# Graph network kernel: tile-end comparisons as ScalarE signs, and GpSimd arithmetic moved

## What is computed

```
h = relu(layernorm(x));  x = x + SAGE(h, src, dst)            # three rounds of mean over neighbours
h = relu(layernorm(x));  x = x + MLP(h, mean attr by src, mean attr by dst)
h = relu(layernorm(x));  x = x + GATv2(h, src, dst)           # attention over incoming edges
h = relu(layernorm(x));  x = x + TP(h, attr, src, dst, type)  # messages of scalars and vectors
```

## Time and profile before

| | us |
|---|---|
| median of 3 runs | 2131.21 (2128.32 to 2134.73) |
| the profiled execution, its own time | 2126.57 |
| its span, first to last instruction | 2124.8 |
| VectorE (DVE) busy in it | 1753.1, 83% |
| TensorE (PE) busy | 1610.9, 76% |
| ScalarE (ACT) busy | 1103.9, 52% |
| GpSimd (POOL) busy | 977.8, 46% |

### The profile page before, as it was taken

One profiled execution on the slowest core, in us unless ns is written; L12 is line 12 of the kernel. 1 busy time (PEld: TensorE's weight loads), 2 busy tenths in 40 slices (PEclk: granted clock), 3 DMA queues, 4 the chain that ended last, 5 costly groups with the idle time before them and its releaser, 6 DMA issues.

```text
span 2124.8 us, 36111 instructions
## 1 busy us (share of the span) xinstructions
PE 1610.9 (76%) x8603; PEld 1273.5 (60%) x8603; DVE 1753.1 (83%) x5207; ACT 1103.9 (52%) x2865; POOL 977.8 (46%) x969
## 2 busy tenths in 40 slices
PE   4656668999998987455777777778377888788786
PEld 3222248888888974344776676677355555555555
DVE  8999988998998977787687787886767778778776
ACT  2787767888997963011423424245434444444443
POOL 4200001111221200577777777760057777777772
PEclk9887779999999998675978869789668787887878
DMA  5665668868886870343222222220021111111111
GB/s 181 197 192 162 181 196 326 308 225 292 323 305 246 327 261 29 110 109 82 71 76 70 79 73 73 75 64 1 32 70 56 54 56 55 55 55 55 55 55 48
DMA packets 168625, 280.38 MB, mean 132 GB/s; under 512 B 23985, under 2 KB 137272, under 8 KB 158578
## 3 DMA queue, kind: packets, MB, share of 16 engines
q1 hardware_dynamic: 132816, 191.61, 27.1%
q0 software_dynamic: 34368, 85.62, 13.4%
q10 hardware_dynamic: 1250, 0.86, 0.2%
HBM read 224.22 MB, written 53.79 MB: 131 GB/s over the span
## 4 chain that ended last, share of the span: by engine, by line
POOL 32%; DVE 13%; issue 12%; PE 11%; ACT 1%; DMA 1%; DVEq 0%; POOLq 0%; ACTq 0%
POOL G L750 19%; POOL AT L738 6%; POOL SCR L738 4%; PE PS L1995 2%; POOL EI L738 2%; PE PS L1996 2%; PE PS L1971 1%; DVE HOT_R L1252 1%; POOL G L738 1%; PE PS L1886 1%; DVE GROUPED_R L1267 1%; DVE GROUPED_R L1261 1%; DVE SCR L1426 1%; PE PS L1770 1%; PE PS L1947 0%
## 5 line engine op out<-in xcount | busy, mean ns | idle before, releaser
L750 POOL DMA_INDIRECT G<-table,src_idx x415 | 406.0, 978 | 167.3 <-issue 125.9
L2102 PE MATMUL PS<-SCR,OH 128*128 128x256 f32 x830 | 281.9, 504 | 107.8 <-DVE SCR L1723 104.7
L2102 PEld LDWEIGHTS PS<-SCR,OH 128*128 128x128 f32 x830 | 201.4, 252 | 160.3 <-DVE SCR L1723 120.7
L1886 PE MATMUL PS<-ALL_R 128*128 128x256 f32 (+3 forms) x2025 | 265.6, 288 | 22.8 <-DVE ALL_R L1314 8.1
L727 POOL DMA_INDIRECT HOT_R<-group_table,EI x56 | 63.3, 1130 | 467.0 <-PE PS L1850 252.3
L1971 PE MATMUL PS<-RX,OH 128*128 x830 | 178.4, 372 | 130.4 <-DVE SCR L1426 80.2
L1886 PEld LDWEIGHTS PS<-ALL_R 128*128 128x128 f32 (+1 forms) x2025 | 250.5, 189 | 25.6 <-issue 9.6
L1971 PEld LDWEIGHTS PS<-RX,OH 128*128 128x128 f32 x830 | 149.3, 248 | 160.2 <-issue 155.4
L738 POOL DMA_INDIRECT AT<-table,src_idx x208 | 213.8, 1028 | 63.4 <-issue 62.2
L957 ACT COPY SCR<-PS 128x640 f32<-128x640 f32 x83 | 57.5, 692 | 287.7 <-PE PS L2077 287.7
L1846 PE MATMUL PS<-HOT_R,GROUPED_R 128*119 128x448 f32 x776 | 181.9, 374 | 9.3 <-DVE G L1272 8.7
(11 more groups left out here) (430 smaller groups left out, 3883.2 us busy)
## 6 DMA issues: line engine op xcount, KB each, us to landing
ALL_R<-adjacency SPq DMA_DIRECT2D x72, 1600.0 KB, 7.5
adjacency<-ALL_R SPq DMA_DIRECT2D x26, 1600.0 KB, 7.6
AT<-dst_in_block SPq DMA_DIRECT2D x103, 128.0 KB
G<-table,src_idx POOLq DMA_INDIRECT x463, 2.5
AT<-table,src_idx POOLq DMA_INDIRECT x208, 2.9
table<-RX SPq DMA_DIRECT2D x10, 320.0 KB, 2.7
radial_rows<-SCR POOLq DMA_DIRECT2D x4, 512.0 KB, 5.7
SCR<-table,src_idx POOLq DMA_INDIRECT x111, 2.8
```

What stands on the lines that cost most here:

```text
L750: pool.indirect_dma_start(G[:, p, q, :], None, tables[i], bass.IndirectOffsetOnAxis(ap=src_idx[:, VB * k + q:VB * k + q + 1], axis=0)).the ...
L1886: ins = pe.matmul(PS[0:m, n % 2, 0:2 * w], (adj(slot) if slot is not None else first_adj(b))(c, m), both(i % 2, c, w), start=j == 0, stop= ...
L2102: ins = pe.matmul(PS[:, q, 0:MSG], OH[:, p, q, :], view(SCR, M_AT + (p * VB + q) * MSG, [[1, MSG]]), start=True, stop=True)
```

## The change

It has four parts.

- The counts: ScalarE writes, for each group, the sign of (visit - 0.5 - end) over 391 ends, five operations for the built visits and four for the others. VectorE sums the signs and makes the count with one affine operation (0.5 x sum + NT/2). The comparisons L1083 and L1114 and the four separate reductions L1115 go; L1097 reads the signs; one reduction over all four groups takes the place of L1115.
- The group table (L710, L712): ScalarE makes it as relu(1 - |row - index|), right behind the signs, and stores it from its own queue. The table's memory overlaps the ring of attributes, so GpSimd waits for that store before its second attribute gather.
- The integer source indices (L706, L707): ScalarE makes them inside its pair loop.
- The marks (L702, L703): GpSimd waits for `kinds_ready` instead of `valid_made`. The kind fills are ordered so that the marks' fills come last, and TensorE waits for the marks only there.

```diff
@@ fills
-        FILLS = attr_fills(range(2)) + [(g, j) for g in range(VG) for j in range(2)] + attr_fills(range(2, VG))
+        FILLS = attr_fills(range(2)) + [(g, j) for j in range(2) for g in range(VG)] + attr_fills(range(2, VG))
@@ gpsimd
             for g in range(VG):
                 at = bass.IndirectOffsetOnAxis(ap=tvi[:, g:g + 1], axis=0)
+                if g == 1:
+                    pool.wait_ge(s("groups_stored"), 16)
                 if g == ATTR_RING:
                     pack_block_words()
                     pool.wait_ge(s("fill_turned"), 5)
...
-            pool.wait_ge(s("valid_made"), 1)
+            pool.wait_ge(s("kinds_ready"), 1)
...
             pool.wait_ge(s("fill_copied_act"), N_FILL)
-            pool.tensor_copy(view(EI, 2 * VW + 3, [[VB, NB]]).bitcast(I32), view(EI, 2 * VW + 3, [[VB, NB]])).then_inc(s("idx_made"), 1)
-            pool.tensor_copy(src_idx[:], EI[:, 0, 0:NV + 1]).then_inc(s("idx_made"), 1)
-            pool.wait_ge(s("idx_made"), 2)
-            for c in range(4):
-                pool.tensor_scalar(view(SCR, HIGH0_AT + c * NSRC, [[1, NSRC]]), iota_h[:, 0:NSRC], bv[:, c:c + 1], None, ALU.is_equal).then_inc(s("groups_made"), 1)
-            pool.wait_ge(s("groups_made"), 4)
-            pool.dma_start(group_table.rearrange("(c p) n -> p c n", p=P), view(SCR, HIGH0_AT, [[NSRC, 4], [1, NSRC]])).then_inc(s("groups_stored"), 16)
...
             pool.wait_ge(s("block_summed"), FIRST)
+            pool.wait_ge(s("idx_made"), 2)
@@ scalar
             act.wait_ge(s("constants_made"), 11)
+            def rank(to, at, n, source):
+
+                for g in range(n):
+                    ins = act.activation(to[:, g], source, ACT.Sign, bias=half_below[:, at + g:at + g + 1], scale=-1.0)
+                ins.then_inc(s("ranked"), 1)
+
+            act.wait_ge(s("scalars_made"), 3)
+            act.wait_ge(s("merge_spread"), 1)
+            rank(built_ranks, VG, GA, PS[:, 2, 0:NT])
+            act.wait_ge(s("ends_spread"), 1)
+            rank(ranks, 0, VG, PS[:, 0, 0:NT])
+            for c in range(4):
+                ins = act.activation(view(SCR, HIGH0_AT + c * NSRC, [[1, NSRC]]), iota_h[:, 0:NSRC], ACT.Abs, bias=bv[:, c:c + 1], scale=-1.0)
+            ins.then_inc(s("groups_made"), 1)
+            act.wait_ge(s("groups_made"), 1)
+            act.activation(view(SCR, HIGH0_AT, [[1, 4 * NSRC]]), view(SCR, HIGH0_AT, [[1, 4 * NSRC]]), ACT.Relu, bias=1.0, scale=-1.0).then_inc(s("groups_made"), 1)
+            act.wait_ge(s("groups_made"), 2)
+            act.dma_start(group_table.rearrange("(c p) n -> p c n", p=P), view(SCR, HIGH0_AT, [[NSRC, 4], [1, NSRC]])).then_inc(s("groups_stored"), 16)
             copy_fills(0, KINDS_AT)
...
+                if j == NORM_FROM + NBLK:
+                    act.copy(view(EI, 2 * VW + 3, [[VB, NB]]).bitcast(I32), view(EI, 2 * VW + 3, [[VB, NB]])).then_inc(s("idx_made"), 1)
+                    act.copy(src_idx[:], EI[:, 0, 0:NV + 1]).then_inc(s("idx_made"), 1)
@@ vector
-            dve.tensor_copy(bv[:], stvi[:])
+            dve.tensor_copy(bv[:], stvi[:]).then_inc(s("scalars_made"), 1)
+            dve.wait_ge(s("scalars_made"), 1)
+            dve.tensor_scalar(half_below[:, 0:VG], tv[:, 0, :], 0.5, None, ALU.subtract).then_inc(s("scalars_made"), 1)
+            dve.tensor_scalar(half_below[:, VG:VG + GA], bv[:], 0.5, None, ALU.subtract).then_inc(s("scalars_made"), 1)
...
-            dve.tensor_tensor(cmp[:, 0:GA], view(PS, 2 * 512, [[0, GA], [1, NT]]), view(bv, 0, [[1, GA], [0, NT]]), ALU.is_lt)
...
-            dve.tensor_reduce(view(stv, 0, [[1, GA]]), cmp[:, 0:GA], AX, ALU.add)
+            dve.wait_ge(s("ranked"), 1)
+            dve.tensor_reduce(stv[:, 0, :], built_ranks, AX, ALU.add)
...
+            done(dve.tensor_scalar(stv[:, 0, :], stv[:, 0, :], 0.5, NT / 2, ALU.mult, ALU.add))
...
-            dve.wait_ge(s("ends_spread"), 1)
-            for g in range(VG):
-                done(dve.tensor_scalar(H[:, g * 4:g * 4 + 4, :].rearrange("p a b -> p (a b)")[:, 0:NT], PS[:, 0, 0:NT], tv[:, 0, g:g + 1], None, ALU.is_lt))
-                done(dve.tensor_reduce(tv[:, 1, g:g + 1], H[:, g * 4:g * 4 + 4, :].rearrange("p a b -> p (a b)")[:, 0:NT], AX, ALU.add))
+            dve.wait_ge(s("ranked"), 2)
+            done(dve.tensor_reduce(tv[:, 1, :], ranks, AX, ALU.add))
+            done(dve.tensor_scalar(tv[:, 1, :], tv[:, 1, :], 0.5, NT / 2, ALU.mult, ALU.add))
...
-            dve.tensor_tensor(va, id_part(1), id_part(2), ALU.not_equal).then_inc(s("valid_made"), 1)
+            done(dve.tensor_tensor(va, id_part(1), id_part(2), ALU.not_equal))
@@ tensor
                     if f == KINDS_AT:
                         pe.wait_ge(s("kinds_ready"), 1)
+                        pe.wait_ge(s("keys_copied"), GA)
+                    if f == KINDS_AT + VG:
                         pe.wait_ge(s("marks_made"), 1)
-                        pe.wait_ge(s("keys_copied"), GA)
```

More of the change, by code:

```diff
@@ L322, in gnn_program @@
         assert 2 * NSRC + LA <= 1280
+        half_below = view(small, 0, [[1, VG + GA]])
+        built_ranks = view(HB, 0, [[NT, GA], [1, NT]])
+        ranks = view(HT, 0, [[NT, VG], [1, NT]])
         def attr_rows(g):
```

## The result

The changed kernel takes **2161.8 us** (median of 6 runs, 2158.9 to 2171.1), the kernel before 2130.0 in the same series: ratio 1.0151, 95% interval 1.0130 to 1.0172. The forecast was 2125.7 us in a range of 2121.5 to 2130.0. The profiled execution took 2162.39 us, 1.9 around its span.

The account below looks back on a forecast made before the run. VectorE's chain was taken to bound the first 300 us; with its wait for ScalarE's square root at visit 12, 5.5 us come off: 2126.57 to 2121.1 us profiled, 2125.7 us (-0.26%) from the median, range 2121.5 to 2130.0.

Parts of the forecast that it names:

- VectorE up to the gathers: VectorE's id preparation: reduction L1097 at 13.6 us, first index gather at 17.8 instead of 19.41, L1116 4.6 us earlier.
- rival B: ScalarE's signs come late by a second table load, 1.28 us: -4.2 us, 2127.0 us; chance 0.14.
- What is late next: VectorE's L1122 waits for TensorE: begins at 23.5 instead of 26.85 us, -3.4, with about 1.5 us idle.
- Marks: GpSimd's products start later, so VectorE's L1182 takes 0.42 us instead of 1.38; visits could start at 50.4 us.
- The other chain: Gathers, fills, ScalarE: first attribute gather at 29.2 us, key copies end at 45.1, square root at 56.9, -3.0 us.
- Where the chains meet: VectorE at visit 12 waits for the square root until 56.95 us; v = 14 at 58.3 instead of 63.80, -5.5 us.
- Rival A: ScalarE's square root is not late, so no wait at visit 12: -7.2 us, 2124.0 us; chance 0.30.
- Rival C: GpSimd held at its second attribute gather by the group table's store: slower, 2137.6 us if it lands at 42.4; chance 0.06.

Follow-up runs that it names:

- e7: Kernel before with only the group table's making and storing moved from GpSimd to ScalarE: 2168.7 us, 1.0192 of the kernel before.
- e17: Changed kernel with the block words' operation moved ahead of the square-root wait and the scales at VectorE's twelfth visit: 2123.3 us, 0.9981 of the kernel before.
- e14: Changed kernel with VectorE pausing at its 14th visit until TensorE has done the visits before: 2124.1 us, 0.9974 of the kernel before.
- e15: Changed kernel with the first norm's scales at VectorE's 30th visit instead of the 12th: 2122.3 us, 0.9970 of the kernel before.
- e5: Changed kernel with GpSimd making and storing the group table again, without its later wait for it: 2126.3 us, 0.9985 of the kernel before.
- e9: Changed kernel with three unused GpSimd comparisons of 448 columns ahead of the first radial gather: 2123.5 us, 0.9962 of the kernel before.
- e16: The kernel of e9 measured once more: 2124.6 us, 0.9982 of the kernel before.
- e10: Changed kernel with one unused GpSimd comparison of 448 columns between first radial gather and store, waiting for std_ready: 2127.2 us, 0.9988 of the kernel before.
- e13: Changed kernel with VectorE pausing at its 66th visit until TensorE has done all 65 before: 2126.2 us, 0.9989 of the kernel before.

## Why the prediction was wrong

**VectorE up to the gathers: right.** L1078's successor begins at 9.63 (said 9.63), the reduction at 13.64 (13.6), the first index gather at 17.81 (17.8), L1116's successor at 20.93 (20.9). The five signs took 2.50 us, the lower end of the bound, and the first began at 10.99, right behind its table load (9.70 + 1.28), and rival B with its late signs is out. (The bound's row was misread: L830 has 415 operations and not five. They are busy 130.4 us in place of 415 x 0.390, which would bring 3.05 us to 2.46.) The drain of about 1380 ns that the Trainium skill ("ScalarE: Activation LUTs", What ACT_TABLE_LOAD costs) states doesn't show there.

**What is late next: right.** 23.41 with 1.51 us of idle (23.5 with about 1.5).

**Marks: right.** 0.43 us (0.42), and the visits began at 50.13 (50.4).

**The other chain: right in kind.** The first attribute gather was at 29.40 (29.2), but TensorE began on its data 7.05 us after the issue began, where it was 6.38 before: 36.45 in place of 35.6. The key copies ended at 45.35 (45.1), the square root at 57.51 (56.9).

**Where the chains meet: right, a little small.** VectorE waited 2.51 us for the square root (1.75 by the forecast's numbers) and went on at 57.54 (56.95); v = 14 began at 58.94 (58.3). The visits ended 5.06 us earlier (5.5). Rival A is out.

**Rival C: out.** GpSimd's second attribute gather followed at 30.65 with no wait for the table.

**The step that failed** is one sentence of the first part: "What follows is tied to the visits' end by waits, not to a clock; I take the shift as carried to the end unchanged." One of these waits is not for the visits but for GpSimd's radial stores, which had ended long before in the kernel of before (the last was issued at 109.2 us) and so looked free. The removal of the four comparisons L710 was costed as a gain alone, for VectorE's visits; of what stands behind them on GpSimd's queue, four gathers and four stores, nothing was costed. They should have had a term of their own. What the runs showed in its place: the first of these stores was held for 227.19 us, three round trips of about 12 us (290.85 to 326.35) came behind it, and VectorE waited 39.27 us for the last of them. The table's move alone, in the kernel before, costs 1.9% (e7). The Trainium skill ("SBUF — State Buffer") names the hazard; that it strikes after and not before could not be read from one trace.

**What the forecast was worth without it.** In e17, the change with two steps exchanged, VectorE goes on behind the visits at 285.85, 6.2 us earlier than before, and the time is lower by 0.19% (0.09 to 0.29), about 4 us of 2128; e14 and e15 stand at 0.26% and 0.30%. The forecast's -0.26% lies among them, and all three are faster than both kernels. That is no proof of its sum: each of the three has a step of its own that moves the visits (the last one-hot ends at 285.93 us in e17, 287.63 in e14 and 284.36 in e15), and the other changed kernels without a long hold (e5, e9, e16, e10, e13) lie between 0.11 and 0.38% under the kernel before. Which of the three is best their intervals don't tell.

## What to carry to other kernels

When work is taken off GpSimd, follow what else stands in its queue: DMA issues beside a long unbroken run of VectorE's can go through in one kernel and be shut out in the next, and a store that "has long been done" is then the last to end. In the trace look at the duration of the issue itself, not only at the landing. Where such issues are needed beside a long run, try what stands directly ahead of the run: here exchanging two small steps or a pause of half a microsecond was enough, and with either the kernel was faster than the one before.

## What was not expected

The state of a run outlives its cause by hundreds of instructions: 0.23 us of work on one partition decides whether a store some us later is held for 227. A pause of 0.51 us (e14, TensorE two visits behind) clears it. GpSimd's arithmetic and the batch statistics beside each other cost nothing: the marks ran from 43.45 to 46.77 us, and from the first statistics to the first visit VectorE took 6.85 us, against 6.86 before.
